# Causal attention: a block's value products between the second and third score product of the next group; GpSimd masks first and splits second

## The reference

```
att = einsum('bhtd,bhsd->bhts', q, k) * 1/sqrt(hd)      # 32 half-heads of 4 columns, T = 1024
att = where(causal, att, -inf)
att = softmax(att, axis=-1)
att = att[:, :, 0] - lambda_full * att[:, :, 1]         # per pair of half-heads
out = einsum('bhts,bhsd->bhtd', att, v)                 # 16 heads of 8 columns
...                                                     # RMS norm, gamma, projection
```

## Time and profile before

| | |
|---|---|
| median of 3 runs | 2138.11 us (2136.7 to 2138.21) |
| profiled execution | 2138.5 us, its span 2136.7 us |
| TensorE busy | 1847.3 us (86%) |
| VectorE busy | 1884.3 us (88%) |
| ScalarE busy | 1108.5 us (52%) |
| GpSimd busy | 1414.5 us (66%) |
| one full job of the attention | 31.14 us |

### The profile page before, as it was taken

One profiled execution on the slowest core, in us unless ns is written; L12 is line 12 of the kernel. 1 busy time (PEld: TensorE's weight loads), 2 busy tenths in 40 slices (PEclk: granted clock), 3 DMA queues, 4 the chain that ended last, 5 costly groups with the idle time before them and its releaser, 6 DMA issues. The chain is left out here.

```text
span 2136.7 us, 35583 instructions
## 1 busy us (share of the span) xinstructions
PE 1847.3 (86%) x14162; PEld 1368.3 (64%) x14226; DVE 1884.3 (88%) x1607; ACT 1108.5 (52%) x1448; POOL 1414.5 (66%) x661
## 2 busy tenths in 40 slices
PE   2799999999756699898998998988989989889877
PEld 1344444444244578777787787777877877778776
DVE  6978887887254899999999999999999999999973
ACT  2267776776611355554545555545455555454540
POOL 5122222222201789889899898898998988989961
PEclk9899999999965899999999999999999999999996
DMA  3300000000000000000000000000000000000000
GB/s 100 64 5 8 8 6 8 9 5 2 1 0 0 1 1 1 2 1 2 1 1 2 1 1 2 1 1 2 1 1 2 1 1 1 2 1 1 1 1 20
DMA packets 10981, 14.46 MB, mean 7 GB/s; under 512 B 4656, under 2 KB 7632, under 8 KB 10672
## 3 DMA queue, kind: packets, MB, share of 16 engines
q1 hardware_dynamic: 9264, 11.31, 2.2%
q10 hardware_dynamic: 1536, 0.63, 0.1%
HBM read 4.57 MB, written 1.05 MB: 3 GB/s over the span
## 5 line engine op out<-in xcount | busy, mean ns | idle before, releaser
L1057 POOL TENSOR_TENSOR b_p_ring<-b_p_ring,b_m 128x2048 f32<-128x2048 f32 (+7 forms) x384 | 1250.9, 3299 | 139.9 <-DVE b_p_ring L969 137.9
L1095 ACT ACTIVATE b_p_ring<-b_p_ring 128x2048 f32<-128x2048 f32 (+7 forms) x384 | 532.7, 1412 | 640.8 <-POOL b_p_ring L1057 640.8
L1158 PE MATMUL b_ps<-k_ident,b_ev_ring 128*128 128x128 f32 (+6 forms) x4608 | 579.7, 276 | 121.7 <-DVE b_ev_ring L1015 121.5
L1015 DVE TENSOR_TENSOR b_ev_ring<-b_p_ring,b_ps 128x2048 f32<-128x2048 f32 (+7 forms) x384 | 634.1, 1655 | 1.7 <-ACT b_p_ring L1095 1.7
L969 DVE TENSOR_TENSOR b_p_ring<-b_ps,b_key 128x2048 f32<-128x2048 f32 (+7 forms) x384 | 634.4, 1660 | 0.0
L1158 PEld LDWEIGHTS b_ps<-k_ident,b_ev_ring 128*128 128x128 f32 (+6 forms) x4608 | 491.3, 135 | 183.3 <-DVE b_ev_ring L1015 159.1
L1158 PE MATMUL b_ps<-k_ident,b_p_ring 128*128 128x128 f32 (+6 forms) x4608 | 567.9, 273 | 19.5 <-ACT b_p_ring L1095 12.5
L1158 PEld LDWEIGHTS b_ps<-k_ident,b_p_ring 128*128 128x128 f32 (+6 forms) x4608 | 504.7, 135 | 26.1 <-ACT b_p_ring L1095 12.8
L564 DVE TENSOR_REDUCE a_negm<-a_ps 128x1 f32<-128x768 f32 (+7 forms) x384 | 354.5, 954 | 89.4 <-PE a_ps L453 88.1
L547 ACT ACTIVATE a_ex<-a_ps 128x512 f32<-128x512 f32 (+3 forms) x768 | 334.3, 497 | 189.3 <-PE a_ps L492 174.9
L384 POOL TENSOR_SCALAR_AFFINE_SELECT a_ex<-a_ex 128x512 f32<-128x512 f32 x128 | 81.6, 638 | 364.4 <-ACT a_ex L547 363.9
(11 more groups left out here) (163 smaller groups left out, 1065.6 us busy)
## 6 DMA issues: line engine op xcount, KB each, us to landing
rk_of_group<-rows_k SPq DMA_DIRECT2D x96, 32.0 KB, 2.0
rq<-rows_q SPq DMA_DIRECT2D x42, 64.0 KB, 2.3
k_wqkv<-in_wqkv SPq DMA_DIRECT2D x1, 2048.0 KB, 8.4
out<-x_all SPq DMA_DIRECT2D x4, 256.0 KB, 2.4
k_wo<-in_wo SPq DMA_DIRECT2D x1, 512.0 KB, 9.2
rq<-rows_q SPq DMA_DIRECT2D x12, 32.0 KB, 1.9
k_w_attn<-in_w_attn ACTq DMA_DIRECT2D x1, 192.0 KB, 2.8
k_reset_max<-in_reset_max ACTq DMA_DIRECT2D x1, 128.0 KB, 4.9
```

The source lines that it names most:

```text
L1015: nc.vector.tensor_tensor(chunk(ev_ring, c), chunk(p_ring, c), over_queries(values(c), c), ALU.mult).then_inc(ev_done.sem, 1)
L1057: nc.gpsimd.tensor_tensor(pc, pc, over_rows(m[:, half].rearrange("p i h -> p (i h)"), c), ALU.subtract).then_inc(shifted.sem, 1)
L1095: nc.scalar.activation(pc, pc, ACT.Exp).then_inc(exp_done.sem, 1)
L1158: last = nc.tensor.matmul(ps[0:width, bank, b // IB * P:(b // IB + 1) * P], rows[:, r, b:hi].rearrange("p i h -> p (i h)"), k["ident"][:], ...
```

## The change

Two edits. In TensorE's loop the value product of group `at - 1` moves from the end of group `at`, behind its four score products and their items, to the place behind the second score product and its items. In GpSimd's loop the mask of group 9 moves ahead of the split for the next job.

```diff
--- before.py
+++ after.py
@@ -409,9 +409,9 @@
             split(0)
             for n in range(JOBS):
                 for at in DIAGONAL:
+                    mask(n, at)
                     if at == 9 and n + 1 < JOBS:
                         split(n + 1)
-                    mask(n, at)
                     if at == 2 and n >= 1:
                         combine(n - 1)
             combine(JOBS - 1)
@@ -521,10 +521,10 @@
                                 break
                             item(*todo[given])
                             given += 1
-                    if at >= 1:
-                        values(n, at - 1)
-                    elif n >= 1:
-                        values(n - 1, G - 1)
+                        if hh == 1 and at >= 1:
+                            values(n, at - 1)
+                        elif hh == 1 and n >= 1:
+                            values(n - 1, G - 1)
             values(JOBS - 1, G - 1)
             turn(JOBS - 1)
```

## The result

| | before | after |
|---|---|---|
| median of the runs | 2137.4 us (4 runs, 2132.86 to 2138.21) | 2212.68 us (4 runs, 2211.85 to 2218.17) |
| ratio, 95% interval | | 1.0362 (1.034 to 1.0384), slower |
| profiled execution (span) | 2138.5 (2136.7) | 2218.17 (2216.4) |
| one full job, first score to first score | 31.14 us | 35.73 us |
| job 0 / job 14 | 29.8 / 34.6 us | 34.6 / 38.9 us |

The changed kernel is 75 us slower; 66 were forecast. The profiled executions differ by 79.7 us, 78 of them in the attention stage, which ended at 584.7 us and now ends at 663.1. The profiled execution of the kernel after is the slowest of its four, 5.5 us above their median, with a mean granted clock of 0.955 where the other three have 0.959 to 0.960.

A forecast was written before the change was run, and what follows sets the result against it. TensorE's in-order stream was taken to bound the attention stage. Jobs 0 to 13 add 57 us, job 14 adds 3 and job 15 adds 6: 66 us on 2138.5 gives 2204, own range 2187 to 2222.

The forecast's parts named there:

- L: Time from the start of a group's fourth score product until a value product may start; 1.38 to 2.14 us in masked groups.
- C: TensorE's work during L in the new order, 0.67 to 1.36 us; each wait is L - C.
- The swap: GpSimd's split begins only when mask 9 ends, giving TensorE's rows product a new wait of 0.6 us a job.
- What pays back: Of 3.0 us of TensorE gaps a job, 2.3 are given back inside the new waits; bounds 0.8 and 2.6.
- Jobs 14 and 15: Last two attention jobs: job 14 grows by 3 us (0 to 6), job 15, without items, by 6 (3 to 9).
- Absorbed: Rival, chance 0.12: waits of groups 3, 4, 10 and the rows don't show, all gaps pay back; 2163 us.
- Clock: Rival, chance 0.10: on top of the waits, one 3.4 us stretch in each job runs at half speed; 2228 us.
- Faster: Rival, chance 0.04: the mask is in time in every group and job 14's 5.4 us of waits vanish; 2126 us.

## Why the prediction was right

The direction, the mechanism and the place were as forecast; the time was 9 us over the forecast, inside the range. Two of its terms were off, in opposite directions, so that the sum is better than its parts. By its steps:

- *L and C.* L held to 0.11: group 8 2.14 forecast, 2.14 measured (362.41 to 364.55), group 9 1.81 and 1.70, group 10 1.54 and 1.61, groups 0, 1 and 3 within 0.05. The mask stayed at 0.63 to 0.64. C was a lower bound, as called, and close in groups 8, 9 and 10, whose waits were forecast 1.05, 1.0, 0.85 and came as 1.04, 0.89, 0.95. In groups 0, 1 and 3 it was 0.15 to 0.19 too small, and their waits came as 0.74, 0.67 and 0.33 where 0.95, 0.85 and 0.5 were forecast. So the waits make 5.9 us a job, not 6.4. TensorE's waits for the mask were forecast as about 110 near 0.8 us. The profile's 81 leave out those of group 8, put down to ScalarE, and the short ones of group 2. By the order of time 112 value products start 0.10 to 0.16 behind a mask's end after standing, for 63.9 us of idle time. That is 0.57 each, and some 0.17 more counted from the start in front.
- *The swap.* Forecast 0.6 for the rows; 0.49 in the trace, 0.46 by taking it back.
- *What pays back.* This term was mis-sized most. I let 2.3 of 3.0 us of gaps vanish, because VectorE would catch up while TensorE stands. With waits of 5.9 the measured 4.59 leaves 1.3 for it, which lies inside the bounds of 0.8 and 2.6; some 0.7 of it is the 0.09 in front of each of eight value products, which was there before. The gaps of groups 4 to 7 stayed whole: from the value product of group 4 to that of group 5 it is 3.63 us before (318.23 to 321.86) and 3.60 after (351.97 to 355.57), in both cases with TensorE's items waiting for VectorE's reduces. VectorE may run only two items behind, so time won in groups 0 to 3 is not carried to group 5, as I read it. Over jobs 0 to 13 the stage grew 64.5 us, where 57 was forecast: 1.0 a job too much paid back, less the 0.5 of waits that did not come.
- *Jobs 14 and 15.* Forecast +3 and +6, measured +4.3 and +9.3, and more than half of the excess of 4.6 is the clock, which I had left to a rival. Job 14 has two long stands, 2.0 us in front of a value product and 2.68 in front of the rows, and behind them the clock was half for 3.4 and 10.2 us, the latter into job 15:

```profile
623.69 0.61 PE L462 MATMUL a_ps<-k_ident_b,a_mrows 128*128 128x128 bf16 x8 [2.68 <-POOL a_mrows L374]
...
629.75 1.94 PE L505 MATMUL a_ps<-a_ex,v 128*32 128x512 f32 x8 [0.74 <-POOL a_ex L384]
```

A value product of 512 columns takes 1.94 there and 1.06 elsewhere. In the kernel with the split early the clock did not fall there, though the rows stood just as long, and job 15 took 34.7 us for 37.5:

```profile
618.18 0.61 PE L464 MATMUL a_ps<-k_ident_b,a_mrows 128*128 128x128 bf16 x8 [2.68 <-POOL a_mrows L374]
620.16:654.86 34.70, 22.64 (x164) 7.53 (x168) 0.78 (x2) 21.47 (x52) 6.75 (x11) 1.00 0.00 0
```

So about 2.8 us are the clock's, and without them job 15 is 6.5 longer than before, near the 6 forecast. The length of a stand alone does not settle whether the clock falls behind it.

*The rivals.* "Absorbed" is out: the waits of groups 3, 4, 10 and of the rows all show. "Clock" is out within the full jobs, which run at 1.00 with eight stands of 0.3 to 1.0 us in each: what the Trainium skill says of small idles (page "TensorE: Matmul & The Clock Gate", section "A second HAM failure mode: psum-queue depth-cycling") does not show here at this size. Where the clock did fall, in job 14 and at the start of job 15, it fell behind single stands of 2.0 and 2.7 us; from 635.5 to 662.7 us, in the rest of job 15, it is 1.00 again with stands of 0.6 to 1.3 us in front of seven value products. "Faster" had one true part: job 14's wait is worth 5 us, but they are had by the items' pace, without the move. That rival's condition, L below C, is met in one masked group, group 11; in group 2 the product still starts 0.15 behind the mask's end.

## What to carry to other kernels

A product that consumes another engine's last step has a cover: the work that stands between its producer and itself in the in-order queue. Before moving it, compare the producer's whole latency (here from the start of the fourth score product over its exponential and the mask to the earliest start of the value product, 2.1 us in group 8) with the work left in between (1.1 us); most of the difference is paid at every turn of the loop. Moves interact through the same cover, so halves of a change need not add up.

Look also at the ends of a loop whose work is dealt out by a quota: the one job with a shorter list dealt it out too slowly, and 5 us were had there by dealing it out at the pace of a full job.

## What the runs showed of the hardware

Handing over from GpSimd's mask to TensorE's matmul takes 0.10 to 0.16 us in every group that waits, and the select costs 0.41 us for 256 elements a partition and 0.63 for 512; if it grows evenly with the elements, about 0.18 is fixed (an estimate from these two). TensorE's clock was at its full 2.4 GHz in all full jobs of the kernel after, with a stand of 0.3 to 1.0 us in front of seven of twelve value products. In job 14 it fell to 1.2 GHz behind stands of 2.0 and 2.7 us (after) and 3.9 us (before). It isn't a matter of length alone: the 2.68 us of the kernel with the split early brought no fall, and in the kernel with the product behind the third score product TensorE stood 1.9 us in front of the rows in every full job, and the clock fell behind it in two of the first fourteen, for 3.4 us each.

```profile
119.30:122.70 3.40, 3.18 (x20) 1.49 (x20) 2.32 (x3) 1.00 (x4) 0.64 (x1) 0.50 0.00 0
153.40:156.80 3.40, 3.40 (x24) 1.57 (x22) 1.22 (x1) 0.55 (x2) 0.41 (x1) 0.51 0.02 5
187.50:191.00 3.50, 2.35 (x25) 1.35 (x27) 1.49 (x2) 0.76 (x4) 0.99 (x5) 1.00 0.02 5
```

These are windows of that kernel, the first two at the lower level, the third from the same place of the job after.
